# Four interleaved units on one core: TensorE's waits and matmuls become separate turns, and all engine orders are written anew

## The reference: what is computed

```python
h = take(L0_tok_W.T, x) * (x != 0)
h = h + retention(ln(h), Wq, Wk, Wv)              # scores * decay mask, no softmax         (ATTN0)
h = h + moe_top2(ln(h), 16 experts, relu, ln)     # 64 -> 128 -> 64, gates by softmax       (MOE0)
h = h + block_attention(ln(h), 2 heads, blocks 8) #                                         (ATTN1)
h = h + moe_top1(ln(h), 32 experts of 16, relu)   #                                         (MOE1)
h = h + linear_attention_ffn(ln(h), 8 heads)      # elu + 1 features, two inner norms       (ATTN2)
h = h + moe_top2(ln(h), 8 experts of 64, gelu)    #                                         (MOE2)
h = h + lru(ln(h))                                # complex diagonal recurrence             (ATTN3)
h = h + binary_moe(ln(h), 8 experts)              # sign(x) . sign(sum of gated weights)    (MOE3)
```

## Time and profile before

| | us |
|---|---|
| median of 3 runs | 938.37 (930.48, 938.37, 938.54) |
| the profiled execution | 928.25 |
| its span | 926.4 |
| TensorE busy | 753.5 (81%) |
| VectorE busy | 538.1 (58%) |
| ScalarE busy | 401.5 (43%) |
| GpSimd busy | 184.7 (20%) |
| mean granted clock of TensorE | 0.72 of 2.4 GHz |

### The profile page before, as it was taken

How to read it: one execution, slowest core, us unless ns; L and a number is a source line. 1 busy time by engine, 2 the same in 40 slices (tenths; PEclk the granted TensorE clock), 3 DMA queues, 4 the chain that set the end, 5 groups by cost and what they waited for, 6 DMA issues and landing times.

```text
span 926.4 us, 8675 instructions
## 1 busy us (share of the span) xinstructions
PE 753.5 (81%) x3058; PEld 323.8 (35%) x3058; DVE 538.1 (58%) x1022; ACT 401.5 (43%) x660; POOL 184.7 (20%) x147
## 2 busy tenths in 40 slices
PE   0347899999998987977976788888988999789965
PEld 0234333433334444444343553433233322411211
DVE  0784665664476565676577666666567436543322
ACT  0142334445443333334343234366554556266643
POOL 6751010100032022230341233211223002100000
PEclk9955699999998996767786657577755556555555
DMA  9110000000000000000000000000000000000000
GB/s 218 40 29 1 1 0 1 1 0 1 0 1 1 1 1 1 1 1 0 1 0 2 0 1 0 1 0 1 0 1 0 1 0 13 11 1 0 0 12 11
DMA packets 7043, 8.24 MB, mean 9 GB/s; under 512 B 5160, under 2 KB 5672, under 8 KB 6824
## 3 DMA queue, kind: packets, MB, share of 16 engines
q1 hardware_dynamic: 5400, 5.09, 2.1%
q10 hardware_dynamic: 576, 1.55, 0.8%
q0 software_dynamic: 1024, 1.05, 0.5%
HBM read 6.44 MB, written 1.25 MB: 8 GB/s over the span
## 4 chain that ended last, share of the span: by engine, by line
PE 70%; DVE 13%; ACT 11%; issue 3%; DMA 1%; POOL 1%; DVEq 0%; ACTq 0%
PE ps L811 13%; PE ps L1011 11%; PE ps L740 9%; ACT room L701 6%; PE ps L741 5%; PE ps L1018 5%; PE ps L834 3%; PE ps L732 3%; PE ps L873 2%; PE ps L991 2%; DVE room L1265 2%; PE ps L750 2%; PE ps L992 1%; PE ps L898 1%; PE ps L965 1%
## 5 line engine op out<-in xcount | busy, mean ns | idle before, releaser
L701 ACT ACTIVATE room<-ps 128x512 bf16<-128x512 f32 x256 | 147.5, 596 | 131.0 <-PE ps L1011 130.6
L1011 PE MATMUL ps<-room,w_rows 32*128 32x512 bf16 x256 | 134.6, 557 | 39.5 <-ACT room L701 34.7
L459 POOL TENSOR_TENSOR inv_std<-var,neg_half 128x8 f32<-128x8 f32 x44 | 74.5, 1696 | 360.8 <-DVE var L1144 360.3
L1444 DVE TENSOR_TENSOR room<-room 128x1024 bf16<-128x1024 bf16 x128 | 92.1, 727 | 85.9 <-ACT room L701 85.8
L607 ACT ACTIVATE room<-ps,kb 128x512 f32<-128x512 f32 x128 | 86.0, 687 | 124.2 <-PE ps L741 124.0
L740 PE MATMUL ps<-xs,up_hi 128*128 128x512 f32 x192 | 108.3, 564 | 27.5 <-DVE room L1265 17.5
L1265 DVE TENSOR_TENSOR room<-ps,room 128x512 f32<-128x512 f32 x128 | 85.3, 686 | 77.3 <-PE ps L834 76.8
L741 PE MATMUL ps<-xs,up_lo 128*128 128x512 f32 x192 | 86.9, 452 | 0.0
L811 PE MATMUL ps<-room,kb 128*64 128x512 f32 x256 | 76.7, 680 | 0.0
L740 PEld LDWEIGHTS ps<-xs,up_hi 128*128 128x128 f32 x192 | 41.3, 215 | 100.2 <-DVE room L1265 38.3
L1011 PEld LDWEIGHTS ps<-room,w_rows 32*128 32x128 bf16 x256 | 24.5, 98 | 146.3 <-ACT room L701 93.7
(11 more groups left out here) (253 smaller groups left out, 1043.9 us busy)
## 6 DMA issues: line engine op xcount, KB each, us to landing
room<-wup SPq DMA_DIRECT2D x2, 782.0 KB, 14.8
out<-h SPq DMA_DIRECT2D x4, 256.0 KB, 2.3
kd<-wd ACTq DMA_DIRECT2D x1, 1007.0 KB, 20.6
kb<-wb SPq DMA_DIRECT2D x1, 893.0 KB, 20.2
room<-binary SPq DMA_DIRECT2D x1, 576.0 KB, 20.9
y<-emb_w,ids_sb POOLq DMA_INDIRECT x32, 3.2
w_rows<-w_bounce SPq DMA_DIRECT2D x2, 192.0 KB
ka<-wa SPq DMA_DIRECT2D x1, 320.0 KB, 3.6
```

What stands on the lines that cost most here:

```text
L459: G.tensor_tensor(inv_std[u][:, :], var[u][:, :], neg_half[:, :], ALU.pow).then_inc(norm_rstd[u], 1)
L701: act.activation(sg[u][:, i % 4, :], bank[0], ACT.Sign).then_inc(m3_s[u], 1)
L1011: pe.matmul(bank[0], w3_rows[rs, P * p:P * (p + 1)], gTb[u][rs, :], start=True, stop=True).then_inc(m3_w[u], 1)
L1444: V.tensor_tensor(pr[u][:, at, :], sg[u][:, at, :], sx[u], ALU.mult).then_inc(m3_p[u], 1)
```

## The change

Every step of TensorE is split: a new `yield` between `pe.wait_ge` and the matmuls makes the wait a turn of its own, so that the string can put the waits of several units first and their matmuls behind them. The down projections lose their own wait (88 of them), since the up before them has waited for the same or a later value; only the last down of a part keeps one. ATTN0's output step waits once for both lanes (`DV_P0B`) where it waited for each. The two kernels do the same computation with the same instructions apart from these waits. All four strings of turns are new.

```diff
@@ turn, and all other steps alike
                         pe.wait_ge(ready, value)
+                        yield
                         for t in tiles:
                             last = pe.transpose(bank[0][:, tile(t)], pair(src[u], t), ident)
@@ ATTN0, output
                     yield
+                    pe.wait_ge(dve_step[u], nth(DV_P0B))
+                    yield
                     for l in lanes:
-                        pe.wait_ge(dve_step[u], nth(DV_P0A + l))
                         for t in tiles:
@@ MOE0
-                    def down(name, layout, weights, k, done, at, last_one):
-                        pe.wait_ge(done[u], at)
+                    def down(name, layout, weights, k, last_one):
                         a = layout[name][0] + D * k
...
                                 pe.wait_ge(mix_hg[u], nth(HG_M0 + n - 1))
+                            yield
                             up(bank[0], "w1_0", e, l).then_inc(mix_z[u], 1)
                             if e and l == 0:
                                 yield
-                                down("w2_0", CB, kb, e - 1, mix_hg, nth(HG_M0 + LANES * e - 1), False)
+                                down("w2_0", CB, kb, e - 1, False)
...
                             pe.wait_ge(mix_h[u], nth(H_MIX0 + n))
+                            yield
                             pe.matmul(bank[0], sel0[rs, e, :], gTb[u][rs, :], start=True, stop=True).then_inc(mix_g[u], 1)
@@ the strings, a line of each
 "POOL"
-        "0 1 2 3 4 0x23 1 0x8 1 0x5 1x2 2x4 3x4 4x4 1x4 2x4 1 2 3x2 1 3x2 1x7 3 1 2 1 4x2 2x5 4x2 3 2x4 1x5 4 3 1 3x4 "
+        "0 1 2 3 4 0x36 1 2 3 4 1 2 1x2 3 4 2x2 3x2 4x2 1x2 2 1x2 2x3 3x2 1 3x2 2 4x4 3 1 4 2 1x7 2 3 1 2 1 2x7 3x3 4 "
 "PE"
-        "0 1 2 3 4 0 1 0x2 1x4 2 1x3 2x4 1x4 2 1x4 2x2 1x2 3 1x5 3 1x3 3 1 2 3 1 2 3 1x2 2 1 2 1 2 1 2x2 1x2 3 1 2 1 "
...
+        "2 1 3 4 2 1x2 3 4 2 1 3 4 2 3 1 3 4 2 1 3 4 2 4 1 3 4 2 1 3 4 2x2 1 3 4 2 1 3 4 2 1x2 3 4 2 1 3 4 2 3 1 3 4 "
...
-        "4x2 3x2 4 3 4x2 3x2 4x2 3 4x2 3 4x49 "),
+        "3x4 4x2 3x2 4x4 3x4 4x2 3x2 4x4 3x4 4x2 3x2 4x4 3x4 4x4 3 4 3 4x3 3x2 4x68 "),
 "DVE"
+        "0 1 2 3 4 0 1x4 0x23 2 3 2 0x4 1 2 3 4 2 3 4x2 2 3 4 3 1x2 4 1x2 2 1 2 1 2 1 2x2 1x2 2 3x2 1x2 4 1 2 1 4 1 3 "
```

More of the change, by code:

```diff
@@ L833, in program @@
                             pe.wait_ge(mix_h[u], nth(H_MIX0 + n))
+                            yield
                             pe.matmul(bank[0], sel0[rs, e, :], gTb[u][rs, :], start=True, stop=True).then_inc(mix_g[u], 1)
                     yield
-                    down("w2_0", CB, kb, E0 - 1, mix_hg, nth(HG_M0 + LANES * E0 - 1), True)
+                    pe.wait_ge(mix_hg[u], nth(HG_M0 + LANES * E0 - 1))
+                    yield
+                    down("w2_0", CB, kb, E0 - 1, True)
                     yield from turn_back(AC_F0)
@@ L901, in program @@
                                 yield
-                                k = LANES * ((m - 1) // 2) + 1
-                                down("w2_1", CD, kd, m - 1, (mix_h, m1_odd)[(m - 1) % 2],
-                                     nth((H_MIX1, 0)[(m - 1) % 2] + k), False)
+                                down("w2_1", CD, kd, m - 1, False)
                     yield
-                    down("w2_1", CD, kd, MT - 1, m1_odd, nth(LANES * ((MT - 1) // 2) + 1), True)
+                    pe.wait_ge(m1_odd[u], nth(LANES * ((MT - 1) // 2) + 1))
+                    yield
+                    down("w2_1", CD, kd, MT - 1, True)
                     yield from turn_back(AC_F1)
@@ L957, in program @@
                                 yield
-                                down("w2_2", CD, kd, m - 1, mix_hg, nth(HG_M2 + LANES * m - 1), False)
+                                down("w2_2", CD, kd, m - 1, False)
                             yield
@@ L967, in program @@
                     yield
-                    down("w2_2", CD, kd, MT - 1, mix_hg, nth(HG_M2 + LANES * MT - 1), True)
+                    pe.wait_ge(mix_hg[u], nth(HG_M2 + LANES * MT - 1))
+                    yield
+                    down("w2_2", CD, kd, MT - 1, True)
                     yield from turn_back(AC_F2)
```

11 lines of the change are left out of this document (10 added, 1 removed), and 94 rows, old and new, of the table TURNS.

## The result

| us | before | after |
|---|---|---|
| median of 4 runs each | 934.42 (929.31 to 938.54) | 844.95 (835.61 to 851.53) |
| ratio, with its 95% interval | 1 | 0.8965 [0.886, 0.9071] |
| span of the profiled execution | 926.4 | 833.8 |
| TensorE busy | 753.5 | 694.6 |
| mean granted clock | 0.72 | 0.80 |

The account below looks back on a forecast made before the run. TensorE's order and clock were taken to set the time. The terms 331 + 469 + 13 + 8 + 115 gave 936, without the 13 and 8 915; midpoint span 926, plus 8: about 934 us, no change, range 898 to 970.

Parts of the forecast that it names:

- Part one, the waits: TensorE's waits: removing waits whose semaphore is up gains zero; a blocked gathered wait costs up to 0.18 us more.
- The 8 us: Cost taken for 112 gathered waits outside MOE0, between bounds of nothing and 20 us plus holding.
- The rival behind them: Outside MOE0, gathered waits hold back ready groups: slower, 950 to 977 us as a time; chance 0.35.
- The rival of the weight loads: MOE0: without waits, weights load ahead, rounds fall to 2.5 us, 29 us less, about 905 us; chance 0.08.
- Part two, MOE0 in step: MOE0: four units run in rounds of 3.0 us, TensorE stays full, 64 rounds take 192 us.
- Part three, the start: Setup to MOE0's end: later first gated product (103 us against 81.7), all units in by 135, MOE0 ends at 331.
- The two stand at the same place at the same time: At MOE0's end, 331 us against 336 before: the early density is paid for by the late start.
- Part four, the middle: From MOE0's end to the last unit's MOE3: 469 us at before's rate of 0.55, plus 13 for VectorE.
- 331 + 469 + 13 + 8 + 115: Forecast span of 936 us: MOE0's end, middle, VectorE's density, gathered waits, tail; midpoint with 915 taken, 926.
- better packing: The middle: units in step give fewer stalls and higher clock, rate 0.59, 32 us less, 902 us; chance 0.28.
- The term for VectorE: From 331 us to unit 1's MOE3: 224 us of VectorE work at 78% take 287 us, 13 more than TensorE asks.
- The tail: From the last unit's start of MOE3 to the end: 115 us, against 103 before, with 58 pair steps left, not 47.

Follow-up runs that it names:

- own waits: The kernel after with every wait again directly ahead of its own matmuls and the down projections' repeated waits kept: 843.73 us, ratio 0.9048.
- e11_gather_only: The kernel before, matmul order kept, with TensorE's waits gathered at 190 places and repeated down waits dropped: 986.72 us beside 933.73 of before.
- The square: Four kernels cut at MOE0's end, start/order behind it: old/old 1010.84 us, old/new 903.94, new/old 970.22, new/new 876.03.
- the replay: Two kernels, new start, strings behind MOE0 taking ready steps first: 860.78 us with units close, 897.12 wide; sorted by targets instead, 977.28 and 960.79.
- e5_rows128: The kernel after with each w3 matmul widened by zero weights from 32 to 128 rows: 810.03 us, ratio 0.8721.
- e7_rows64: The kernel after with each w3 matmul widened by zero weights from 32 to 64 rows: 851.82 us, ratio 0.9146.

## Why the prediction was wrong

**Part one, the waits: right for this change, with one gap.** A wait whose semaphore is up costs nothing that shows: own waits and the 88 dropped ones make no difference (843.73 us with, 844.95 without). The 8 us that I set for the 112 gathered waits outside MOE0 did not come. The rival behind them is real all the same, at 0.2 to 0.3 us each in `e11_gather_only`, about where I had put the point at which it decides (0.25). In after it did not happen; I gave it 0.35 since I could not tell from the string whether the gathered steps fall due together. The rival of the weight loads is out: the round of MOE0 did not shrink.

**Part two, MOE0 in step: right.** The timeline of after, TensorE in MOE0:

```profile
199.22 1.08 PE L833 MATMUL ps<-room,kb 128*64 128x512 f32 x4
...
200.88 0.40 PE L757 MATMUL ps<-xs,up_lo 128*128 128x512 f32 x1
201.21 0.39 PE L858 MATMUL ps<-room,sel 64*128 64x512 bf16 x1
...
202.19 0.65 PE L833 MATMUL ps<-room,kb 128*64 128x512 f32 x2
```

From down to down it is 202.19 - 199.22 = 2.97 us, forecast 3.0; up to gate is 201.21 - 200.88 = 0.33 us, with the wait gone, as in the earlier trace rows. The exposed 0.1 us is still there. By the Trainium skill (TensorE: Matmul & The Clock Gate, Part 2, step 1) loads are pulled ahead of running matmuls; the trace shows no more of that without the wait than with it.

**Part three, the start: right in its times, wrong in what I read from them.** The first up was forecast at 100 to 110 us and comes at 94, the last unit's at 120 (forecast 135), MOE0 ends at 330 to 334 (forecast 331), and the work done up to then is 236 us at full clock, 12 more than before had from 53 us to 336. "The two stand at the same place at the same time" is true of the amount, within those 12 us. But at that moment the four units of after lie 57 us apart and those of before 181. I compared sums and dropped the shape. The square prices the new start at 28 to 41 us behind a cut, and the replay prices closeness at 36.

**Part four, the middle: the step that failed.** I carried the middle's rate of before, 0.55, over to after, and let only VectorE's density change it, downwards. The rate is 0.66. In the sum 331 + 469 + 13 + 8 + 115 the first and the last term held (330 and 110 measured); the middle, 469 + 13 + 8 = 490 us, took 394. There are two errors. The first is that a rate was taken for a property of the kernel, though it is a result of the order: in the middle of before VectorE stood at one unit's step while another unit's was ready for 80 us, in after for 15, and ready steps first, against sorted ones, moved the whole kernel by 64 to 116 us. The second is that I held the clock fixed. It rose from 0.70 and 0.64 to 0.83 and 0.78 in the first two stretches of the middle, and it shortens every matmul, so 25 us less of idle time came with 68 us less of busy time. Whether less waiting is what raised it was not tried by itself. I had written the rival for this, better packing, but at 0.59 and 902 us; its mechanism was right, its size was short by 60 us of span, since I moved it by the spread that I saw among the stretches of the earlier trace rows instead of letting the clock answer. The term for VectorE was wrong three times over. The 13 us don't follow from their own figures: 160 us of TensorE's work at the rate of 0.55 take 291 us, more than the 287 that VectorE was to need. The 224 us of VectorE's work were overcounted: it is busy for 188.38 us from 330 us to unit 1's MOE3. And the cap of 78% with gaps was an extrapolation from a stretch in which VectorE was not the bound: it is busy 80% of the 235 us without them.

**The tail: right.** 110 us against 115 forecast; the clock with three units in MOE3 is 0.53. Not foreseen is what the windows view of after shows for 586 to 627 us, where units 1 and then 2 are in MOE3 with the others' steps between their pairs:

```profile
586.00:627.00 41.00, 39.49 (x158) 13.27 (x156) 29.20 (x45) 34.21 (x61) 5.28 (x4) 1.00 0.00 1
658.00:709.00 51.00, 49.90 (x153) 17.42 (x151) 32.21 (x45) 31.21 (x59) 5.69 (x4) 0.53 0.00 1
```

TensorE is over 96% busy in both, and the clock is 1.00 in the one and 0.53 in the other.

## What to carry to other kernels

A rate read from a stretch belongs to the order that ran in it. Before it is carried to a new order, ask how often each engine, the second busiest too, stood at one chain's step while another chain's was ready, and don't hold the clock fixed: here each microsecond less of TensorE's idle time came with nearly three less of busy time. Gathered waits cost nothing in one order here and 0.2 to 0.3 us each in another: price them by whether the steps fall due together. Where TensorE is full at half its clock, look at the shape of its matmuls: four times the rows, with zeros, made this one faster by 35 us, 44 behind MOE0. And compare two kernels stage by stage from a common event: a late start of 17 us hid what 64 rows do and made the gap between the orders look smaller than it is.

## What the runs showed of the hardware

- A stretch in which TensorE is 98% busy can be granted 0.53 (658 to 709 us of after). From unit 3's first w3 matmul to unit 4's the clock was 0.53 with w3 over 32 rows, 0.75 over 64 and 1.00 over 128; from there to the end 0.51, 0.51 and 0.83. How the clock is decided between these shapes stays open.
- A matmul's weight load took as long over 32 rows as over 128: 99 ns in after (735 to 800 us), 96 in `e5_rows128` (730 to 780 us).
- VectorE's small setup operations, 0.19 us apart in most traces, stood up to 1.4 us apart from 33 to 46 us in `e5_rows128` and `e7_rows64`, whose edit doesn't touch them. Nothing in the traces says why.
- A hard cut between two parts costs 77 us in one order and 30 in another, more than many edits are worth. A kernel that joins two orders needs its control with the same cut.
